# Linear attention in one model kernel: joined logits product, key sums in three products, one masked product handed from VectorE to GpSimd, a turn of its own for the last sequence

## The reference

```python
q, k, v = split(layernorm(x) @ w.T, 3)              # each B, T, 128
k_exp = exp(k * scale) + 1e-6
k_norm = cumsum(k_exp, axis=T)
qs = softmax(q * scale, per head) / k_norm
S_t = S_{t-1} + k_exp_t[:, None] * v_t[None, :]     # per head, 8 x 8
y_t = qs_t @ S_t
x = x + y @ w_out
```

## Time and profile before

| | |
|---|---|
| median of 3 runs | 770.77 us (769.87 to 771.87) |
| time of the profiled execution | 770.8 us |
| its span, first to last instruction | 769.0 us |
| PE busy | 641.4 us (83%) |
| DVE busy | 537.2 us (70%) |
| ACT busy | 369.8 us (48%) |
| POOL busy | 345.6 us (45%) |

### The profile page before, as it was taken

The page is one execution under the profiler, slowest core; times in us unless marked ns, Lnnn a source line. Parts: engine busy times, 40 slices in busy tenths (PEclk is TensorE's granted clock), DMA queues, the critical chain, the costliest instruction groups (busy, mean ns, idle before and its releaser), DMA issues.

```text
span 769.0 us, 14796 instructions
## 1 busy us (share of the span) xinstructions
PE 641.4 (83%) x4415; PEld 401.7 (52%) x4415; DVE 537.2 (70%) x1801; ACT 369.8 (48%) x793; POOL 345.6 (45%) x491
## 2 busy tenths in 40 slices
PE   1479899997504999999889788899999999999895
PEld 1246666665301588877666554454545454544453
DVE  7368888887695013225467868889898888988554
ACT  0433222330360422224722247777777777767873
POOL 0176655563103766465854444334334343433341
PEclk9999999998955999999999999999999999999997
DMA  9400000000040122133563132030304040400011
GB/s 299 122 1 0 1 1 0 0 1 0 1 136 21 50 42 32 28 62 72 86 97 36 15 61 64 4 63 5 58 9 60 8 62 5 64 5 2 17 57 41
DMA packets 40730, 32.48 MB, mean 42 GB/s; under 512 B 3984, under 2 KB 37312, under 8 KB 40656
## 3 DMA queue, kind: packets, MB, share of 16 engines
q1 hardware_dynamic: 31472, 24.10, 13.9%
q0 software_dynamic: 7840, 6.86, 6.1%
q10 hardware_dynamic: 1344, 0.62, 0.3%
HBM read 13.60 MB, written 8.13 MB: 28 GB/s over the span
## 4 chain that ended last, share of the span: by engine, by line
PE 62%; DVE 20%; issue 8%; ACT 4%; POOL 2%; DMA 1%; SPq 0%; DVEq 0%; ACTq 0%; POOLq 0%
PE bank L2095 8%; PE bank L1225 7%; DVE masked L1691 6%; PE wide L1217 6%; PE wide L2082 5%; PE bank L2029 5%; PE wide L652 4%; PE wide L653 3%; PE bank L624 3%; DVE prod L402 2%; PE wide L1237 2%; PE bank L2107 2%; PE wide L634 2%; DVE st L305 1%; PE wide L2029 1%
## 5 line engine op out<-in xcount | busy, mean ns | idle before, releaser
L1888 ACT ACTIVATE pexp<-wide 128x512 f32<-128x512 f32 (+2 forms) x384 | 181.1, 536 | 75.3 <-PE wide L2082 73.5
L1691 DVE CUSTOM_DVE_ANT_0 masked<-bank,mask_qk 128x384 f32<-128x384 f32 (+3 forms) x376 | 164.1, 481 | 34.2 <-PE bank L2029 32.7
L1819 POOL TENSOR_SCALAR_AFFINE_SELECT pexp<-pexp 128x256 f32<-128x256 f32 x256 | 106.4, 429 | 166.2 <-ACT pexp L1888 164.6
L2082 PE MATMUL wide<-qT,kTe 128*128 128x256 bf16 (+3 forms) x512 | 121.7, 301 | 6.3 <-ACT pexp L1888 3.5
L2029 PE MATMUL bank<-kTm,qT 128*128 128x384 bf16 (+3 forms) x376 | 89.7, 301 | 17.6 <-DVE mx L1691 13.0
L1167 ACT ACTIVATE hT<-wide,b1T 128x512 f32<-128x512 f32 x64 | 43.9, 686 | 111.5 <-PE wide L1217 111.5
L967 POOL DMA_INDIRECT x_dram<-yg,row_u x40 | 63.7, 1594 | 67.4 <-DVE yg L1019 59.5
L976 POOL DMA_INDIRECT x_row<-xln_dram,row_u x64 | 62.9, 983 | 52.5 <-DVE slot_tok L843 33.6
L2095 PE MATMUL bank<-pexp,vx 128*32 128x512 f32 (+3 forms) x1024 | 84.3, 441 | 2.3 <-POOL pexp L1819 2.3
L1691 DVE CUSTOM_DVE_ANT_0 masked<-wide,mask_qk 128x512 f32<-128x512 f32 (+3 forms) x136 | 64.7, 499 | 15.2 <-PE wide L2029 14.9
L578 POOL TENSOR_TENSOR kv<-kx,qv 128x1024 f32<-128x1024 f32 x32 | 62.3, 1949 | 25.3 <-PE wide L653 25.2
(11 more groups left out here) (285 smaller groups left out, 1072.5 us busy)
## 6 DMA issues: line engine op xcount, KB each, us to landing
qT<-qp SPq DMA_DIRECT2D x126, 64.0 KB
x_sb<-in_L_attn_x SPq DMA_DIRECT2D x8, 256.0 KB, 6.7
w_sb<-in_L_ffn_w SPq DMA_DIRECT2D x1, 2048.0 KB, 12.9
xln_dram<-hT SPq DMA_DIRECT2D x8, 256.0 KB, 2.3
out_x<-x_sb SPq DMA_DIRECT2D x7, 256.0 KB, 2.3
x_dram<-x_sb SPq DMA_DIRECT2D x5, 256.0 KB, 2.7
...
```

Source lines behind the costliest of these rows:

```text
L1691: ins = nc.vector.tensor_tensor_reduce(out=masked[:, n % 4, at], in0=bank_of(n)[:, at], in1=mask_qk[:, T - w:T], scale=1.0, scalar=LEAST, ...
L1819: nc.gpsimd.affine_select(out=pexp[:, at, :, 0:P], in_=pexp[:, at, :, 0:P], pattern=[[0, 2], [1, P]], compare_op=ALU.is_ge, fill=0.0, base ...
L1888: nc.scalar.activation(pexp[:, exp_slot(b, 2 * step + h // 2), h % 2:h % 2 + nh, 0:w], scores_bank(b, m)[:, 0:nh * w].rearrange("p (h t) - ...
L2082: ins = nc.tensor.matmul(scores_bank(b, m)[:, hh * w:(hh + 1) * w], kTe[:, par, j * P:(j + 1) * P], qT[:, b % QB, 4 * qd + h + hh, j * P:T ...
```

## The change

1. **Logits join the projection.** `wor` becomes columns 128 to 135 of `wo_sb`; one product per tile has 136 columns, two tiles to a bank of `wide2` (`projected`). The four 8-column products go. The residual and the logits read the two banks; the next key sums and states, which use these banks, now wait for the logits step.
2. **Three key-sum products.** `tri` over all four tiles in one 512-column product, `ones` times tile 0 for tile 1, and `ones` times two sums of tiles that POOL forms (`k_sum`, two adds of 128x128) for tiles 2 and 3 in one 256-column product.
3. **Third product on POOL.** In turns 1 to 6 ACT copies the sums of tile 2 out of PSUM (`sums_2`, 128x1024), the sums of tile 3 wait for this copy in place of DVE's product, and POOL multiplies. DVE's reduce of tile 2 moves behind the state. Residual, logits and statistics stand together ahead of product 3.
4. **First and last turn.** In turn 0 DVE does all four products. The last turn is written anew: the sums of odd tiles go into a second pair of banks (`wide0`, those that the front used), and residual, logits and statistics of sequences 6 and 7 come at its end.

The core of the diff on DVE and the layout of PSUM:

```diff
-        bank = {i: psum(f"bank{i}", 1) for i in (0, 1, 2, 7)}
-        wide, wide2 = psum("wide", 2), psum("wide2", 2)
+        bank = {i: psum(f"bank{i}", 1) for i in (0, 7)}
+        wide0, wide, wide2 = psum("wide0", 2), psum("wide", 2), psum("wide2", 2)
+        bank[1], bank[2] = wide0[:, 0:512], wide0[:, 512:1024]
...
-        a_kv, a_cum, a_prod, a_red = A("outer", NT), A("outer_sums_psum", NT), A("q_times_sums", NT), A("y_intra", NT)
+        a_kv, a_cum, a_prod, a_red = A("outer", NT), A("outer_sums_psum", NT), A("q_times_sums", NT - 1), A("y_intra", NT)
+        a_cc, a_pp = A("third_sums_copied"), A("q_times_third_sums")
...
+        projected = wide2[:, :].rearrange("p (a n) -> p a n", a=2)[:, :, 0:2 * (D + E)].rearrange("p a (k n) -> p a k n", k=2)
...
+        sums_at = lambda k, last: wide0 if last and k % 2 else wide
...
-        def dve_lin_prod(dve, b, k):
...
+        def dve_lin_prod(dve, b, k, last=False):
...
+            done = a_pp if k == BY_POOL else a_prod
...
-                wide[:, :].rearrange("p (h m l) -> p h m l", l=L, m=L),
-                qs[:, k, :].rearrange("p (h l) -> p h l", l=L).unsqueeze(2).broadcast_to([P, HEADS, L, L]), ALU.mult).then_inc(a_prod.sem, 1)
+                sums_at(k, last)[:, :].rearrange("p (h m l) -> p h m l", l=L, m=L),
...
+            by_bank = x_sb[:, b, :, :].rearrange("p (a k) d -> p a k d", a=2)
+            nc.vector.tensor_tensor(by_bank, by_bank, projected[:, :, :, 0:D], ALU.add).then_inc(a_x.sem, 1)
...
+            by_bank = lg[:, b].rearrange("p (a k) e -> p a k e", a=2)
+            nc.vector.tensor_tensor(by_bank, by_bank, projected[:, :, :, D:D + E], ALU.add).then_inc(a_lg.sem, 1)
...
-        def dve_lin_turn(dve, b, par, tail=True, front=True):
+        def dve_lin_turn(dve, b, par, tail=True):
             dve_lin_prod(dve, b, 0)
-            if front:
-                dve_lin_qmax(dve, b + 1, 1 - par)
+            dve_lin_qmax(dve, b + 1, 1 - par)
             dve_lin_reduce(dve, b, 0)
             dve_lin_prod(dve, b, 1)
             dve_lin_reduce(dve, b, 1)
             if tail:
                 dve_lin_residual(dve, b - 1)
-            dve_lin_prod(dve, b, 2)
-            dve_lin_reduce(dve, b, 2)
-            if tail:
                 dve_lin_logits(dve, b - 1)
                 dve_lin_stats(dve, b - 1)
+            else:
+                dve_lin_prod(dve, b, BY_POOL)
             dve_lin_prod(dve, b, 3)
-            if front:
-                dve_lin_qsum(dve, b + 1)
-                dve_lin_den(dve, b + 1)
+            dve_lin_qsum(dve, b + 1)
+            dve_lin_den(dve, b + 1)
             dve_lin_state(dve, b)
+            dve_lin_reduce(dve, b, 2)
             dve_lin_reduce(dve, b, 3)
...
+        def dve_lin_last_turn(dve, b):
+            dve_lin_prod(dve, b, 0, last=True)
+            dve_lin_prod(dve, b, 1, last=True)
+            dve_lin_reduce(dve, b, 0)
+            dve_lin_prod(dve, b, 2, last=True)
+            dve_lin_reduce(dve, b, 1)
+            dve_lin_prod(dve, b, 3, last=True)
+            dve_lin_state(dve, b)
+            dve_lin_reduce(dve, b, 2)
+            dve_lin_reduce(dve, b, 3)
+            for before in (b - 1, b):
+                dve_lin_residual(dve, before)
+                dve_lin_logits(dve, before)
+                dve_lin_stats(dve, before)
```

On ACT, POOL and PE (the lambdas, renamed tiles and the `last=True` arguments of unchanged calls are left out):

```diff
+        def act_lin_sums(act, b):
+
+            act.wait_ge(a_cum.sem, a_cum.at(b, BY_POOL + 1))
+            act.wait_ge(a_pp.sem, a_pp.at(b, 0))
+            nc.scalar.activation(sums_2[:, :], wide[:, :], ACT.Copy).then_inc(a_cc.sem, 1)
...
+            if tail and front:
+                act_lin_sums(act, b)
...
+        def pool_lin_key_tiles(pool, b, par):
+
+            pool.wait_ge(a_kxe.sem, a_kxe.at(b, 1))
+            pool.wait_ge(a_kn.sem, a_kn.at(b, 0))
+            nc.gpsimd.tensor_tensor(k_sum[:, 0, :], kx[:, par, 0, :], kx[:, par, 1, :], ALU.add).then_inc(a_k2.sem, 1)
+            pool.wait_ge(a_k2.sem, a_k2.at(b, 1))
+            nc.gpsimd.tensor_tensor(k_sum[:, 1, :], k_sum[:, 0, :], kx[:, par, 2, :], ALU.add).then_inc(a_ks.sem, 1)
...
+        def pool_lin_prod(pool, b):
+            pool.wait_ge(a_cc.sem, a_cc.at(b - 1, 1))
+            pool.wait_ge(a_qs.sem, a_qs.at(b, 1))
+            pool.wait_ge(a_red.sem, a_red.at(b, 1))
+            nc.gpsimd.tensor_tensor(
+                prod[:, BY_POOL % 2, :].rearrange("p (h m l) -> p h m l", l=L, m=L),
+                sums_2[:, :].rearrange("p (h m l) -> p h m l", l=L, m=L),
+                qs[:, BY_POOL, :].rearrange("p (h l) -> p h l", l=L).unsqueeze(2).broadcast_to([P, HEADS, L, L]),
+                ALU.mult).then_inc(a_pp.sem, 1)
...
+                pool_lin_key_tiles(pool, b + 1, 1 - par)
             pool_lin_outer(pool, b, par, 3)
+            if tail and front:
+                pool_lin_prod(pool, b)
             if front:
                 pool_lin_logits(pool, b + 1, 1 - par)
...
+            pool_lin_turn(pool, 0, 0, tail=False)
+            pool_lin_turn(pool, 1, 1)
+            with nc.gpsimd.Fori(1, B // 2 - 1) as i:
...
-            for k in range(NT):
-                for j in range(k):
-                    nc.tensor.matmul(psN[:, k * D:(k + 1) * D], ones, kx[:, par, j, :], start=j == 0, stop=False)
-                ins = nc.tensor.matmul(psN[:, k * D:(k + 1) * D], tri, kx[:, par, k, :], start=k == 0, stop=True)
...
+                pe.wait_ge(a_lg.sem, a_lg.at(b - 1, 0))
+            nc.tensor.matmul(psN[:, :], tri, kx[:, par].rearrange("p k d -> p (k d)"), start=True, stop=False)
+            nc.tensor.matmul(psN[:, D:2 * D], ones, kx[:, par, 0, :], start=False, stop=False)
+            pe.wait_ge(a_ks.sem, a_ks.at(b, 1))
+            nc.tensor.matmul(psN[:, 2 * D:4 * D], ones, k_sum[:, :, :].rearrange("p k d -> p (k d)"),
+                             start=False, stop=True).then_inc(a_kn.sem, 1)
...
+            if b_before is not None:
+                pe.wait_ge(a_lg.sem, a_lg.at(b_before, 1))
...
-            pe.wait_ge(a_prod.sem, a_prod.at(b, k))
...
+            if last and k == 1:
+                pe.wait_ge(a_qv.sem, a_qv.at(b, NT))
+            elif last:
+                pe.wait_ge(a_prod.sem, a_prod.at(b, max(0, k - 1)))
+            elif k <= BY_POOL:
+                pe.wait_ge(a_prod.sem, a_prod.at(b, k))
+            elif tail:
+                pe.wait_ge(a_cc.sem, a_cc.at(b - 1, 1))
+            else:
+                pe.wait_ge(a_pp.sem, a_pp.at(b, 1))
+            at = sums_at(k, last)
...
-            pe.wait_ge(a_lg.sem, a_lg.at(b, 0))
...
+                pe.wait_ge(a_st.sem, a_st.at(b, 1))
+            else:
+                pe.wait_ge(a_lg.sem, a_lg.at(b, 0))
+                pe.wait_ge(a_st.sem, a_st.total(B))
+            pe.wait_ge(s_prep_v.sem, s_prep_v.total(9))
...
-                ins = nc.tensor.matmul(psN[:, k * D:(k + 1) * D], yT[:, k * P:(k + 1) * P], wo_sb[:, :],
+                ins = nc.tensor.matmul(projected[:, k // 2, k % 2, :], yT[:, k * P:(k + 1) * P], wo_sb[:, :],
...
-            pe.wait_ge(s_prep_v.sem, s_prep_v.total(9))
...
-                ins = nc.tensor.matmul(psR[:, k * E:(k + 1) * E], yT[:, k * P:(k + 1) * P], wor[:, :],
-                                       start=True, stop=True)
-            ins.then_inc(a_lgp.sem, 1)
...
+        def pe_lin_last_turn(pe, b, par):
+            pe_lin_outer_sums(pe, b, 0, last=True)
+            pe_lin_outer_sums(pe, b, 1, last=True)
+            pe_lin_yT(pe, b - 1)
+            pe_lin_outer_sums(pe, b, 2, last=True)
+            pe_lin_qsT(pe, b, False)
+            pe_lin_outer_sums(pe, b, 3, last=True)
+            pe_lin_states(pe, b, par, b - 2)
+            pe_lin_project(pe, b - 1, last=True)
+            pe_lin_yT(pe, b)
+            pe_lin_project(pe, b, last=True)
```

More of the change, by code:

```diff
@@ L482, in act_lin_xT @@
             act.wait_ge(a_qkv.sem, a_qkv.at(b, 0))
-            nc.scalar.activation(xT[:, :], psT[:, :], ACT.Copy).then_inc(a_xT.sem, 1)
+            nc.scalar.activation(xT[:, :], psLT[:, :], ACT.Copy).then_inc(a_xT.sem, 1)
         def act_lin_kx_qv(act, b, par, k, first=False):
@@ L582, in pool_lin_outer, with pool_lin_turn @@
                 ALU.mult).then_inc(a_kv.sem, 1)
-        def pool_lin_turn(pool, b, par, front=True):
+        def pool_lin_prod(pool, b):
[7 more added lines that the diff above has]
+                ALU.mult).then_inc(a_pp.sem, 1)
+        def pool_lin_turn(pool, b, par, tail=True, front=True):
             pool_lin_qs(pool, b)
@@ L601, in lin_pool @@
             pool_lin_outer(pool, 0, 0, 1, first=True)
-            with nc.gpsimd.Fori(0, B // 2 - 1) as i:
+            pool_lin_turn(pool, 0, 0, tail=False)
+            pool_lin_turn(pool, 1, 1)
+            with nc.gpsimd.Fori(1, B // 2 - 1) as i:
                 pool_lin_turn(pool, 2 * i, 0)
@@ L647, in pe_lin_states, with pe_lin_outer_sums @@
             ins.then_inc(a_stp.sem, 1)
-        def pe_lin_outer_sums(pe, b, k):
+        def pe_lin_outer_sums(pe, b, k, tail=True, last=False):
```

(43 more changed lines are left out.)

46 lines of the change are left out of this document (22 added, 24 removed).

## The result

The changed kernel takes **763.98 us** (median of 6 runs, 759.6 to 765.0) against 770.9 us (6 runs, 769.4 to 771.87) before: ratio 0.9899, 95% interval 0.9868 to 0.993, faster by 1%. The forecast was 762.8, in a range of 758.8 to 767.5. The profiled execution took 759.96 us with a span of 758.2, near the lower end of the six, so its gain of 10.8 us is more than the usual one.

What follows compares the result with a forecast made beforehand. PE's loop of waits in the middle turns was taken as the bound, with DVE's becoming longer after the change. Gains of 0.4 (first turn), 5.5 (six middle turns) and 2.1 (last), 8.0 us from 770.8, gave 762.8 us, range 758.8 to 767.5.

Steps and rivals of the forecast that it cites:

- Period: Middle turns of the linear attention, from reciprocal's end to reciprocal's end: 18.97 us in place of 19.89.
- Key sums: PE's loop, middle turn: three products (1.51 us) in place of ten (2.24) save 0.73 us.
- Logits: PE's loop, middle turn: sums of tile 2 could start at 92.10 in place of 92.38, saving 0.28 us.
- Copy for product: PE's loop, between sums of tiles 2 and 3: ACT's copy and hand-over, 1.17 us in place of 1.37, save 0.20.
- This loop is now the longer one by 0.3 us: moving the reduce is what caps the gain: Middle turn: DVE's loop, with a second reduce between reciprocal and yT, takes 18.97 us against PE's 18.68.
- POOL's product: Third product in middle turns: 1.95 us on POOL, bounds to 2.54, far end 3.90; up to 2.5 us it is hidden.
- Last turn: From the last reciprocal's end to the end of the statistics: 22.3 us in place of 24.47, gaining 2.1 us.
- 3.0 less at full: Rival, last turn: yT and the sums behind it run at full clock, 3.0 us less, 759.8 us; chance 0.20.
- 6.53 us: Last turn: time from yT's start to the product at half clock, kept from the earlier trace; a middle turn needs 3.5.
- First turn: Turn 0: DVE waits 0.41 us for the key sums before den, so shorter key sums give 0.4 us.
- Slower rival: PE's clock falls in the six middle turns, 3.0 us more each, 18 in all: 781 us; chance 0.05.
- The rule that I cited: Trainium skill: PE can pause so often between groups of matrix products that the clock gate swings between its two levels.

Runs made afterwards that it cites:

- second trace: The changed kernel, unaltered, profiled again in a later set of runs: median 762.37 us, ratio 0.9887 to the kernel before.
- experiment 4: Changed kernel with the reduce of tile 2 cut to one head in turns 1 to 6: one execution 759.77 us, turns of 18.82 us.
- experiment 5: Changed kernel with POOL's third product done twice, the first time into a tile nobody reads: one execution 772.64 us, turns of 21.23 us.
- first trace: The changed kernel, unaltered, in its first profiled execution: 759.96 us, span 758.2.

## Why the prediction was right, and where not

- **The total is right in part by luck.** It was summed as 0.4 at the start, 5.5 in six turns and 2.1 in the last. In the second trace (762.58 us, close to the forecast) the second reciprocal ends 2.2 us later than before, six turns give 6.0 and the last stretch 4.0: 7.8 in all, against 8.0. The start, which was to give and took, and the last turn, which gave twice its share, nearly cancel.
- **Period.** Forecast 18.97, measured 18.89; six turns gained 6.0 us (5.5).
- **Key sums** 0.73: measured 0.67 and 0.62. **Logits** 0.28: measured 0.14, because I had read a start wrongly. The chain in the earlier trace rows puts the sums of tile 2 at 92.38, which is the modelled end of the logits product; their own record starts at 92.24, 0.14 us after the 92.10 at which they could have started:

```profile
91.42 0.96 PE L690 MATMUL bank<-wor,yT 128*128 128x8 f32 x8
92.24 1.11 PE L652 MATMUL wide<-kv,cst 128*128 128x512 f32 x2
```

In all six turns the sums start 0.27 or 0.28 us after product 1, of which 0.14 is the hand-over. **Copy for product** 0.20: measured 0.15, and 0.22 (19.04 - 18.82) where the second reduce does not stand in the way.
- **"This loop is now the longer one by 0.3 us: moving the reduce is what caps the gain"**: wrong in size. PE's loop was put at 18.68 and is 18.8, by the 0.14 us of the logits, and DVE's is longer by 0.07. Without the second reduce the turn would have been 18.82 (experiment 4). The time came out because the loops are 0.1 apart.
- **POOL's product** at 1.95 us: it takes 2.35, inside the bounds; POOL's slack was found as worked out, and experiment 5 prices it.
- **Last turn**, 22.3 us at half clock, 3.0 less at full: at full clock it is 18.85, with a fallen clock 20.5 (both to the end of the statistics). The mis-sized term is the 6.53 us taken over from yT's start to the product: it is 187.60 - 182.38 = 5.2 in the second trace. The clock was at half from yT's start on before, and here only from 183 us on:

```profile
182.38 0.46 PE L741 MATMUL bank<-cst,y_in 128*128 128x128 f32 x2 [2.45 <-DVE y_in L421]
...
187.60 1.22 DVE L409 TENSOR_TENSOR prod<-wide,qs 128x1024 f32<-128x1024 f32 x1 [1.38 <-PE wide L718]
```

- **First turn**, 0.4 us: this failed. Turn 0 takes 18.15 and 20.00 us where it took 18.04. In the first trace the first reciprocal comes 0.7 us earlier than before, so that 0.6 are gained all the same; in the second it comes 0.2 later, and 2.2 are lost by the second reciprocal. Turn 0 takes 19.85 to 20.28 us in five of the eight traces with three key products on one pair of banks and in none of the three with ten. That does not show the key products to be the cause. The kernel before with the three products alone had a turn 0 of 18.24. All five long ones also had late q, k, v products (0.7 to 1.0 us), which come ahead of the key products and differ between two executions of one kernel; with ten key products only the kernel with joined logits had them late, and its turn 0 took 18.04. What sets how long the clock stays down stays open.
- **Slower rival**, the clock in the middle turns: granted 1.00 in them in both traces of the change, with 12% idle. The rule that I cited for it showed nothing there. It is near all the same: with pauses of 2.0 us, in experiment 5, the clock fell in two middle turns, at 1.6 us each in place of the 3.0 of the forecast.

The spread of 759.6 to 765.0 is thus 12.3 us gained up to the layernorm in the first trace, less up to 2.8 at the start, 1.6 in the last turn and 1.6 in a later stage, in some executions each. How often each of the three comes is not known, since two executions of this kernel were traced.
